# A four-layer transformer on one core: maxima and contexts turned by identity products in column tiles, with an order of steps written anew

## The reference

```python
m = silu(cond) @ ada_w + ada_b                      # shifts, scales and gates
q, k, v = split((ln(x) * (1 + scale_a) + shift_a) @ qkv_w + qkv_b)
x = x + gate_a * (softmax(q @ k.T / 4) @ v @ proj_w + proj_b)
q2 = ln(x) @ q_w + q_b                              # layer 2 with gamma and beta
k2, v2 = split(context @ kv_w + kv_b)               # layer 3: ln(context)
x = x + softmax(q2 @ k2.T / 4) @ v2 @ cp_w + cp_b
h = gelu((ln(x) * (1 + scale_m) + shift_m) @ fc1_w + fc1_b)
x = x + gate_m * (h @ fc2_w + fc2_b)
```

## Time and profile before

| | us |
|---|---|
| runs (3): median, lowest, highest | 2457.8, 2456.67, 2457.94 |
| the profiled execution | 2459.47 |
| its span, first to last instruction | 2457.7 |
| PE busy | 2394.8 (97%) |
| DVE busy | 1875.6 (76%) |
| ACT busy | 1263.5 (51%) |
| POOL busy | 466.9 (19%) |

### The profile page before, as it was taken

One profiled execution on the slowest core, in us unless ns is written; L12 is line 12 of the kernel. 1 busy time (PEld: TensorE's weight loads), 2 busy tenths in 40 slices (PEclk: granted clock), 3 DMA queues, 4 the chain that ended last, 5 costly groups with the idle time before them and its releaser, 6 DMA issues.

```text
span 2457.7 us, 93436 instructions
## 1 busy us (share of the span) xinstructions
PE 2394.8 (97%) x41326; PEld 1616.7 (66%) x41326; DVE 1875.6 (76%) x3532; ACT 1263.5 (51%) x1810; POOL 466.9 (19%) x510
## 2 busy tenths in 40 slices
PE   6889999999999999999999999999999999999998
PEld 3556666666666666666666666666666666666666
DVE  5777788888888888887777777778777777777763
ACT  1444555555555555554554554555555545545544
POOL 0112211211121211111111111212212212212121
PEclk8989999999999999999999999999999999999999
DMA  6431222222222222222221221222231322312211
GB/s 214 133 113 61 99 86 78 78 88 85 80 84 84 91 93 76 93 89 72 70 88 60 85 78 55 88 88 70 94 108 60 106 70 76 100 60 89 85 40 39
DMA packets 143669, 209.27 MB, mean 85 GB/s; under 512 B 14978, under 2 KB 75588, under 8 KB 143268
## 3 DMA queue, kind: packets, MB, share of 16 engines
q1 hardware_dynamic: 143268, 203.30, 24.2%
HBM read 58.34 MB, written 4.39 MB: 26 GB/s over the span
## 4 chain that ended last, share of the span: by engine, by line
PE 91%; DVE 5%; issue 1%; ACT 1%; DMA 1%; SPq 0%; POOL 0%; POOLq 0%; DVEq 0%; ACTq 0%
PE ring L1220 38%; PE ring L1216 13%; PE o_acc L1380 12%; PE score L1327 11%; PE score L1349 9%; PE ring L1174 4%; PE score L1354 3%; DVE row_max_F L1008 3%; DVE row_max_G L1008 2%; ACT probs L1147 1%; DMA gate_now_P<-gate_rows 0%; SPq L693 0%; PE ring L1256 0%; DMA q_F<-q_parts 0%; DMA k_G<-k_parts 0%
## 5 line engine op out<-in xcount | busy, mean ns | idle before, releaser
L1147 ACT ACTIVATE probs<-score 120x2048 f32<-120x2048 f32 (+1 forms) x320 | 601.6, 1880 | 302.2 <-PE score L1354 273.5
L1008 DVE TENSOR_REDUCE row_max_F<-score 128x8 f32<-128x2048 f32 x192 | 438.6, 2285 | 88.8 <-PE score L1327 86.2
L1158 ACT ACTIVATE h_t<-ring,cols 128x256 f32<-128x256 f32 x384 | 160.6, 470 | 415.5 <-PE ring L1220 289.3
L1008 DVE TENSOR_REDUCE row_max_G<-score 128x16 f32<-128x1920 f32 x128 | 276.2, 2158 | 65.4 <-PE score L1327 65.4
L1220 PE MATMUL ring<-x_t_E,w_fc 128*32 128x256 f32 x4736 | 279.6, 380 | 0.0
L1030 DVE STREAM_TRANSPOSE o_turned<-o_acc 128x512 f32<-128x512 f32 x224 | 159.4, 712 | 127.7 <-PE o_acc L1380 127.2
L1220 PE MATMUL ring<-w_fc,h_t 128*32 128x256 f32 x3680 | 215.4, 380 | 0.0
L1220 PEld LDWEIGHTS ring<-x_t_E,w_fc 128*32 128x32 f32 x4736 | 149.0, 110 | 100.2
L1380 PE MATMUL o_acc<-probs,v_self 128*17 128x256 f32 x3072 | 203.8, 383 | 0.4 <-DVE o_turned L1030 0.4
L817 POOL TENSOR_TENSOR x<-x,gated 128x512 f32<-128x512 f32 x48 | 61.2, 1274 | 612.1 <-DVE gated L1049 611.8
L1349 PE MATMUL score<-q_F,k_F 32*128 32x256 f32 x3072 | 166.1, 302 | 9.0 <-ACT probs L1147 4.5
(11 more groups left out here) (154 smaller groups left out, 4155.7 us busy)
## 6 DMA issues: line engine op xcount, KB each, us to landing
k_F<-k_parts SPq DMA_DIRECT2D x192, 256.0 KB, 2.5
q_G<-q_parts SPq DMA_DIRECT2D x128, 256.0 KB, 2.6
k_G<-k_parts SPq DMA_DIRECT2D x256, 120.0 KB, 2.1
q_F<-q_parts SPq DMA_DIRECT2D x96, 256.0 KB, 3.4
gate_now_P<-gate_rows SPq DMA_DIRECT2D x48, 256.0 KB, 3.9
gate_now_E<-gate_rows SPq DMA_DIRECT2D x48, 256.0 KB, 3.7
x<-in_x_dram SPq DMA_DIRECT2D x16, 256.0 KB, 4.0
out_dram<-x SPq DMA_DIRECT2D x16, 256.0 KB, 2.4
```

The lines of the kernel that those rows point to most:

```text
L1008: nc.vector.tensor_reduce(dst, src, AX.X, ALU.max).then_inc(row_max_ready[r].sem, 1)
L1147: nc.scalar.activation(probs[v % 2][0:keys, :, :], score[0:keys, :].rearrange("p (h q) -> p h q", h=2 * GROUPS), ACT.Exp, scale=SCALE).the ...
L1158: last = nc.scalar.activation(h_t[:, c, :], ps[:, c % 2 * NT:(c % 2 + 1) * NT], ACT.Gelu_apprx_tanh, bias=col(m, "fc1", c))
```

## The change

M and C are no longer in `TURNED`. They take the mode of their place: at full size they are transposes as before, in columns they are products with the identity as the moving operand, 32 columns of the source stationary at a time. Three waits are added or made explicit (ACT's LN of role P waits until the q and k before it are done, PE's V for its own x). The tables `START`, `TURN`, `WITH_L1` and `TAIL` are written anew; a line or two of them stand here.

```diff
-TURNED = ("LN", "C", "M", "ZT", "ZC", "ZX")
+TURNED = ("LN", "ZT", "ZC", "ZX")
 IN_COLUMNS = ("ZM", "ZG")
...
                     if r == "P":
+                        q_psum[r].wait_before(act, m, n)
+                        k_psum.wait_before(act, m, n)
                         v_psum.wait_before(act, m, n)
...
                     for k in range(KC):
-                        last = transpose(ps[:, k * S:(k + 1) * S], src[0:S, k * P:(k + 1) * P], S)
+                        if tiles:
+                            last = product(ps[:, k * S:(k + 1) * S], src[0:S, k * P:(k + 1) * P], ident[0:S, 0:S], tiles, start=True, stop=True)
+                        else:
+                            last = transpose(ps[:, k * S:(k + 1) * S], src[0:S, k * P:(k + 1) * P], S)
                     last.then_inc(c_psum.sem, 1)
...
                 elif step == "V":
                     if n == 0:
                         pe.wait_ge(w_v_loaded, full_done(m))
+                    pe.wait_ge(x_t_ready[r].sem, x_t_ready[r].after(m, n))
...
                     for t in range(TT):
-                        last = transpose(ps[:, t * P:(t + 1) * P], max_parts[r][:, t, :], P)
+                        if tiles:
+                            last = product(ps[:, t * P:(t + 1) * P], max_parts[r][:, t, :], ident[:, :], tiles, start=True, stop=True)
+                        else:
+                            last = transpose(ps[:, t * P:(t + 1) * P], max_parts[r][:, t, :], P)
                     last.then_inc(m_psum[r].sem, 1)
...
 WITH_L1 = """
-P.ST
-1G.S0 P.ld 1R.ld 1R.RES E.H0 1R.C
-F.S0 P.V P.V.d P.LN R.C c.ld
-F.S1 f.PV3 E.H1
...
+E.RES
+1G.S0 E.H0
+F.S0 f.PV3 P.V P.ld P.V.d
+F.S1 P.LN 1R.C E.H1 R.C
```

More of the change, by code:

```diff
@@ L49 @@
 TURN = """
[L50 to L61, removed]
+P.gld
+F.S0 f.PV3 E.H0 f.O1
+F.S1 E.H2 E.H1 E.RES
+F.S2 P.V P.LN P.V.d R.C
+F.S3 P.ld A.PR F.X E.H3 A.PR.d
@@ L62 @@
+G.S0 F.M P.Q
+G.S1 B.PR E.F20a
+F.T0 P.RES P.K G.M P.Q.d
+F.T1 G.X c.NC B.PR.d F.PV0 p.N P.K.d E.F20b R.N
+G.T0 E.F20b.d F.PV1 P.ST R.KV F.O0 e.N
+G.T1 G.PV0 R.A e.A R.RES E.F21a
+F.T2 E.F21b G.O0 E.F21b.d R.KV.d R.LN E.gld c.ld p.A
+F.T3 c.AC G.PV1 G.O1 R.Q F.PV2 e.LN R.Q.d
 """.split()
 WITH_L1 = """
-P.ST
-1G.S0 P.ld 1R.ld 1R.RES E.H0 1R.C
-F.S0 P.V P.V.d P.LN R.C c.ld
-F.S1 f.PV3 E.H1
[L68 to L80, removed]
+E.RES
+1G.S0 E.H0
+F.S0 f.PV3 P.V P.ld P.V.d
+F.S1 P.LN 1R.C E.H1 R.C
+F.S2 E.H2 f.O1 E.H3
+F.S3 1R.LN A.PR
+1G.S1 B.PR A.PR.d E.F20a 1G.X 1p.NC F.X
+G.S0 B.PR.d E.F20b P.RES E.F20b.d P.gld p.N P.ST P.K
@@ L81 @@
+G.S1 1G.M P.K.d P.Q R.N P.Q.d 1R.ld G.X 1R.RES
+1G.T0 E.F21a F.M R.A
+1G.T1 p.A E.gld c.ld 1G.PV0 1G.O0 E.F21b
+F.T0 1p.AC E.F21b.d 1G.O1 1G.PV1 1R.KV 1p.N e.N e.A G.M
+F.T1 F.PV0 1R.KV.d 1p.A 1R.Q 1R.Q.d
+G.T0 F.PV1 R.LN e.LN
+G.T1 G.PV0 F.O0 R.KV G.O0
+F.T2 G.PV1 R.Q R.RES
+F.T3 G.O1 F.PV2 R.KV.d R.Q.d 1B.PR 1B.PR.d
 """.split()
 START = """
-P0.N Z0.ZT P0.A P0.ld Z0.ZL Z0.ZC P0.LN Z0.ZM Z0.ZA Z0.ZX P0.K P0.Q P2.ld W0.raw W0.proj P0.V W0.v P1.ld P1.LN
-W0.self P1.N P0.K.d P1.A P0.V.d P0.Q.d P2.N P2.A Z0.ZG Z1.ZA P1.K
@@ L86 @@
[L86 to L94, removed]
-F1.S3 P2.Q
[L96 to L113, removed]
+P0.N Z0.ZC P0.ld Z0.ZL Z0.ZA P2.ld P0.A Z1.ZL Z0.ZT W0.raw P1.ld Z0.ZM W0.proj P0.LN Z0.ZX W0.v W0.self Z1.ZC
+Z0.ZG P0.K P0.Q R0.ld P0.V P3.ld P0.K.d P1.N P0.Q.d Z0.ZS1 Z0.ZS0 P0.V.d P1.LN Z1.ZA P1.V W0.cross P1.A P1.Q
@@ new lines @@
+P2.N P1.V.d
+F0.S0 R0.C P1.K Z2.ZL P1.Q.d
+F0.S1 P1.K.d
+F0.S2 Z2.ZC
+F0.S3 P2.A F0.X
+F1.S0 Z1.ZM P5.ld P2.LN
+F1.S1 P3.N R1.ld F0.M P2.K P0.gld
+F0.T0 Z2.ZA W0.v2
+F1.S2 F0.PV0 Z2.ZG P2.K.d
+F0.T1 P3.A Z2.ZM
+F1.S3 P2.Q
+F0.T2 F0.PV1 F1.X P0.RES P2.Q.d
+F0.T3 Z3.ZA W0.fc2 F0.PV2 F0.O0 F0.O1 F1.M
+F1.T0 Z3.ZL F0.PV3 W0.cpb Z1.ZX
+F1.T1 A0.PR Z2.ZS0 A0.PR.d
+F2.S0 R0.N F1.PV0
+F2.S1 F1.PV1 R0.A R0.KV P4.ld R0.KV.d
+F1.T2 R0.LN Z3.ZM R1.C
+F2.S2 P2.V P1.RES P3.LN
+F2.S3 W0.cp Z2.ZS1 F2.X R0.Q P1.gld P2.V.d R0.Q.d P2.gld F1.O0 P4.N F1.O1
@@ L114 @@
+F1.T3 F2.M F1.PV2
+F2.T0 F1.PV3
+G0.S0 F2.PV0 P3.K
+F2.T1 A1.PR A1.PR.d P3.K.d
+G0.S1 G0.X P3.Q P3.Q.d R1.N P4.A F2.PV1 W0.fc1 Z2.ZX F2.O0 R0.RES G0.M
+G0.T0 R1.KV R1.A
+G0.T1 G0.PV0 R1.KV.d R2.ld R1.LN Z3.ZC W1.l1
+F2.T2 Z3.ZS1 R1.RES P2.RES R3.ld G0.O0 G0.O1 G0.PV1 R1.Q R1.Q.d
+F2.T3 Z3.ZG Z3.ZS0 F2.PV2 Z3.ZX
 """.split()
 TAIL = """
[L116 to L140, removed]
+F15.S0 R14.C P15.V
@@ new lines @@
+F15.S1 E11.H0 E11.RES E11.H1 P15.V.d
+F15.S2 F14.PV3 P11.ST R14.KV
+F15.S3 R14.KV.d E11.H2 B12.PR F15.X F14.O1
+G13.S0 B12.PR.d E11.H3 A14.PR
+G13.S1 F15.M E11.F21a
+F15.T0 A14.PR.d E11.F20a R15.NC G13.X G13.M P15.gld
+F15.T1 F15.PV0 R14.N E11.F20b E12.N
+G13.T0 F15.PV1 E11.F21b R14.A R15.AC
+G13.T1 R14.LN E12.LN E12.A G13.PV0
+F15.T2 E11.F20b.d R14.RES R14.Q G13.PV1 F15.O0 E11.F21b.d G13.O0
+F15.T3 E12.H0 E12.RES F15.PV2 P15.RES R14.Q.d F15.PV3 E12.gld G13.O1 E12.H1 F15.O1
+G14.S0 A15.PR B13.PR A15.PR.d E12.H2 R15.N B13.PR.d R15.A E12.H3
@@ new lines @@
+G14.S1 R15.LN E13.N R15.C E12.F20a G14.X R15.KV E12.F20b R15.Q E13.A R15.KV.d G14.M E12.F21a
+G14.T0 E12.F21b E12.F20b.d R15.Q.d E13.LN R15.RES
+G14.T1 G14.PV0 E13.H0 G14.O0 E12.F21b.d
+G15.S0 G14.PV1 G14.O1 E13.H2 E13.H1
+G15.S1 E13.H3 B14.PR G15.X E13.gld E13.F20a E14.gld E13.F20b B14.PR.d G15.M E13.F21a E14.N
+G15.T0 P12.ST E13.RES E13.F21b E15.gld E13.F20b.d E14.A E13.F21b.d E14.LN
+G15.T1 G15.PV0 E14.H0 G15.PV1 E14.RES G15.O0 E14.H1 E14.H2 E14.H3 B15.PR E14.F20a E14.F20b P13.ST E14.F21a
+E15.LN G15.O1 B15.PR.d E14.F21b E15.H0 E15.H1 P15.ST E15.H2 P14.ST E15.N E15.H3 E15.F20a E14.F20b.d E15.F20b
@@ L141 @@
+E15.A E15.RES E14.F21b.d E15.F21a E15.F20b.d E15.F21b E15.F21b.d
 """.split()
```

## The result

| | before | after |
|---|---|---|
| runs: median (lowest to highest), us | 2457.9 (2456.7 to 2459.2) | 2486.3 (2485.5 to 2492.1) |
| the profiled execution, its span | 2459.5, 2457.7 | 2492.1, 2490.3 |
| PE busy in it | 2394.8 | 2418.1 |

A forecast was written before the change was run, and what follows sets the result against it. TensorE (PE), hardly ever idle in the turns, was taken to bound the kernel. Terms 11.5 + 12.9 + 3.8 + 1.2 = 29.4 us took the profiled 2459.47 to 2488.9; the median, 1.7 lower, gave 2487, range 2474 to 2502.

The forecast's parts named there:

- 25 plain turns: Turns without layer 1: seven of twelve stretches change, +0.46 us a turn to 45.67, +11.5 us in all.
- 15 turns with layer 1: Turns with layer 1: eight stretches change, +0.86 us a turn to 58.7, +12.9 us in all.
- start, turns 3 to 5 and 21, tail: The rest of the kernel: +3.8 us for the start, +1.2 us for these turns and the tail.
- The price of M: Each turned maximum in columns: 16 records take 0.44 us where two transposes took 0.22, 24.2 us over 110 steps.
- Rival (a): M in columns costs no more than the transposes, as four tiles run side by side; 2472.5 us, chance 0.09.
- rival (e): M in columns costs four times the transposes, 0.87 us; 2534 us, chance 0.03.
- The seven stretches: Changed stretches of a plain turn, priced from measured contents: together 24.99 us before and 25.45 after.
- The reduction's bound behind 1G.S0: In a layer-1 turn, work there is 2.90 us but the reduction needs 3.44; PE's wait grows from 0.2 to 0.54.
- [M, Q] ahead of 1G.T0: Stretch of a layer-1 turn, forecast at 3.44 us because the reduction bounds it.
- the eight stretches: Changed stretches of a layer-1 turn: together 28.39 us before and 29.25 after.
- rival (d): Layer-1 turns: a slower DVE pass behind normalization delays LN's ring buffer, up to 1 us a turn; 2500 us, chance 0.15.
- The start: Ahead of the first score: V and Q replace K and w_raw's load waits; first score at 36, +3.8 us net.

The follow-up runs named there:

- second profile: The changed kernel run again without any edit, for another profile on the chip shared with later runs; median 2487.6 us, 1.0119 of the kernel before.
- old order with columns: The changed kernel with the four order tables of the kernel before, M and C still in column tiles; 2478.8 us, 1.0083 of the kernel before.
- Statistics earlier: The changed kernel with e.N, DVE's statistics of the MLP's norm, moved ahead of 1G.O1 in WITH_L1; 2479.1 us, 1.0083 of the kernel before.
- new start with the old turns: The changed kernel with WITH_L1, TURN and TAIL of the kernel before, C and M back in TURNED; 2458.6 us, 1.0001 of the kernel before.
- transposes: The changed kernel with C and M back in TURNED, so full-size transposes in the new order; 2479.8 us, 1.0090 of the kernel before.
- mended order: The changed kernel with transposes, e.N ahead of 1G.O1, 1R.C behind H0, and sample 1's V and Q behind the first scores; 2468.0 us, 1.0040 of before.

## Why the prediction was right

The total (2487 against 2486.3) is closer than its terms are:

| term | predicted | first profile | second profile |
|---|---|---|---|
| 25 plain turns | +11.5 | +11.1 | +10.9 |
| 15 turns with layer 1 | +12.9 | +19.4 | +19.4 |
| start, turns 3 to 5 and 21, tail | +5.0 | +2.1 | -1.4 |
| sum | +29.4 | +32.6 | +28.9 |

- *The price of M* (0.44): right. The rows show it: 0.46 with the way in, and 0.43 more for 16 more records. The old order with columns agrees (21 us more), though 43 contexts turned to columns add to it there. Rival (a) would have made the old order with columns 2457, rival (e) 2525; it took 2478.8. The factor of four of the Trainium skill (TensorE: Matmul & The Clock Gate, Terms) does not hold for this pair: 0.46 against 0.27 with the way in each, and a slope of 0.43 for the products against 0.22 for the two transposes, is a factor of two. The comparison is of identity products in column tiles with transposes at full size; no run has the products at full size.
- *A plain turn* (45.67): 45.61. The 45.67 starts from 45.21, the mean of the 25; the usual turn was 45.17, so the step forecast as +0.46 came as +0.44. The seven stretches were forecast as 3.25, 3.44, 3.21, 3.57, 3.63, 3.27 and 5.08, and came as 3.24, 3.45, 3.20, 3.56, 3.63, 3.27 and 5.08. It worked because a stretch of a given content costs the same anywhere, so those of before could be put together anew.
- *The reduction's bound behind 1G.S0*: right, 3.44 with PE idle for `row_max_G`. That it also ends the stretch of [M, Q] ahead of 1G.T0 was wrong by 0.05: that took 3.39, and the context had to be 3.50 where it took 3.41. Together the eight stretches came to 29.10 instead of 29.25.
- *A turn with layer 1* (58.7): this step failed. Without the wait it is 58.57; with it 59.18. I had listed what could wait more, and rival (d) put a new wait in this turn on DVE's row behind its norm passes, up to 1 us a turn. The engine, the turn and the size were right and the place was not: not an LN short of its ring buffer but a PV short of `o_acc`. What I had missed is in the table: e.N and e.A side by side, with an instruction of POOL between them, in a row of DVE that is full. The sum had put this wait at nothing. Statistics earlier settles the cause, with 8.5 us (14 turns at 0.61).
- *The start* (+3.8, first score at 36): too much. The first score came at 33.65 and 33.77, and with the same table between 29.2 and 34.1 in five other kernels, where it was 30.56; the new start with the old turns is worth 0 to within 0.1%. Taking V and Q from ahead of it brought it to 27.16, 2.1 before the earliest of those, but the three stretches behind it then took 15.05 where they had taken 9.81 in that kernel (transposes).

So the size of the total is partly luck: 6.5 too little in the turns with layer 1 against 3 to 6 too much in the start and tail. The sign and the greater part of it are not.

Where the 28 to 30 us are, by the experiments: the late `o_turned` 8.5 (statistics earlier), M and C in columns 7.9 (transposes; 6.4 by the turns), the context behind LN 3.3 (by the turn), and 10.0 that the mended order still has over before. The turns give 11.0 of that, 0.28 x 25 = 7.0 in the plain ones and 0.27 x 15 = 4.0 in the others, nearly all of it PE's work and not waits; turn 6 began 2.3 earlier there. In a plain turn with transposes it is [V, LN, C] at 3.24 for the 3.14 of [H2, LN], and an E.LN that needs a change to full size of its own at the end of [PV, Q, PV], where before both LN's shared a stretch with F21b. That this change is what costs is worked out from the stretches; no run takes it alone.

On changes of tiling mode, [K, M] is the clean comparison: 3.05 at full size (1581.37 to 1584.42 in PE's timeline of before), 3.21 in columns (1593.93 to 1597.14 in the old order with columns), where M itself has 0.22 more. So leaving full size gives 0.06 back. Over the whole kernel in the old order the 111 column M's add 0.22 each, 24.4, and the 43 contexts 5.6 (an estimate, at the 0.13 of the one stretch above). Of these 30 us 21 stayed; what came back or was hidden in waits for the maxima is under 0.1 for each of the 107 stretches that left full size. The drain at a change that the Trainium skill names (TensorEngine Tiling (Array Packing), Key Properties) was thus no reason to give up the transposes: the score steps are in row tiles, and the changes at both ends of a stretch stay whatever is in it.

## What to carry to other kernels

Where one engine bounds a loop and its stretches repeat, price a new order by putting measured stretches together, with the bound of each waiting engine as a floor; here that was right to 0.1 us a turn, before a run, but for one wait on another engine. Then walk the other engines' rows of the new order as closely: two steps that pass through a third engine (statistics, rstd, application) should not stand side by side on an engine whose row is full (0.61 us a turn here). And before giving a cheap operation a dearer form to save a mode change, measure what the change costs in the stretches that there are.
